# Two semaphore signals of TensorE in each attention step, scores ahead of the next keys, and ten buffers for 0/1 matrices

## The reference

```
q_i = (x @ idx_wq).reshape(B_, L_, N_IDX_HEAD, D_HEAD)
k_i = x @ idx_wk
s_i = jax.nn.relu(jnp.einsum('bthd,bsd->bths', q_i, k_i))
I = jnp.einsum('bths,h->bts', s_i, idx_w)
...
_, idx = jax.lax.top_k(I, kk)
...
key_c = (c_kv @ W_uk)[bi, idx].reshape(B_, L_, kk, N_HEAD, D_HEAD)
value = (c_kv @ W_uv)[bi, idx].reshape(B_, L_, kk, N_HEAD, D_HEAD)
...
scores = (jnp.einsum('bhld,bhlkd->bhlk', q_c, k_c) + jnp.einsum('bhld,blkd->bhlk', q_r, key_r)) * scale
attn = jax.nn.softmax(scores.astype(jnp.float32), axis=-1).astype(v.dtype)
out = jnp.einsum('bhlk,bhlkd->bhld', attn, v)
...
return out @ W_out
```

## Time and profile before

| | |
|---|---|
| time, 3 runs | 932.55 us median (932.08 to 933.81) |
| the profiled execution | 933.06 us, span 931.2 us in the trace |
| busy share of the span | PE 90%, DVE 73%, ACT 55%, POOL 53% |
| costliest group of POOL | L621, the gathers into the ring, 284.6 us in 284 instructions |
| the chain that ended last | PE 51%, POOL 17%, DVE 12%, issue 10%, ACT 6%, DMA 2% |
| mean granted clock of TensorE | 0.91 of full speed |

### The profile page before, as it was taken

How to read it: one execution, slowest core, us unless ns; L and a number is a source line. 1 busy time by engine, 2 the same in 40 slices (tenths; PEclk the granted TensorE clock), 3 DMA queues, 4 the chain that set the end, 5 groups by cost and what they waited for, 6 DMA issues and landing times.

```text
span 931.2 us, 17728 instructions
## 1 busy us (share of the span) xinstructions
PE 837.1 (90%) x5742; PEld 489.5 (53%) x5742; DVE 679.2 (73%) x1979; ACT 508.3 (55%) x1463; POOL 492.2 (53%) x738
## 2 busy tenths in 40 slices
PE   6867999999999999999999998778989987889786
PEld 3334556565556565656565654445549532535353
DVE  1879899788698998999899986413222279686864
ACT  5455756654567788877877854434432244243231
POOL 4620038877757777777777777777410425202120
PEclk9768999999999999999999986857597999899898
DMA  7310122222101111111111111191025200000000
GB/s 246 73 23 1 30 49 57 46 54 48 36 20 28 29 24 31 26 24 30 27 26 26 29 24 29 23 256 24 21 75 162 54 18 0 1 0 12 11 1 23
DMA packets 59642, 39.98 MB, mean 43 GB/s; under 512 B 27072, under 2 KB 51360, under 8 KB 59424
## 3 DMA queue, kind: packets, MB, share of 16 engines
q1 hardware_dynamic: 44064, 23.40, 10.0%
q0 software_dynamic: 12800, 14.15, 7.6%
q10 hardware_dynamic: 2688, 1.31, 0.5%
HBM read 33.31 MB, written 5.55 MB: 42 GB/s over the span
## 4 chain that ended last, share of the span: by engine, by line
PE 51%; POOL 17%; DVE 12%; issue 10%; ACT 6%; DMA 2%; SPq 0%; POOLq 0%; DVEq 0%; ACTq 0%
POOL G L621 11%; PE psK L745 6%; PE psI L655 6%; PE psS L1753 3%; PE psK L641 3%; PE psP L807 3%; ACT R L903 2%; PE psP L814 2%; PE psS L781 2%; PE psP L796 2%; POOL spacer L620 2%; PE psS L784 2%; POOL w_first L621 2%; DVE G L1971 2%; PE psM L718 1%
## 5 line engine op out<-in xcount | busy, mean ns | idle before, releaser
L621 POOL DMA_INDIRECT G<-key_rows,idx x284 | 284.6, 1002 | 180.0 <-DVEq L1142 82.6
L655 PE MATMUL psI<-kiT,qiT 64*128 64x512 f32 (+5 forms) x320 | 91.7, 595 | 16.1 <-ACT R L903 15.8
L641 PE MATMUL psK<-cst 128*128 128x512 bf16 x315 | 93.7, 408 | 4.9 <-ACT KT L1007 4.9
L1031 ACT ACTIVATE PT<-psP 128x256 f32<-128x256 f32 x128 | 48.4, 378 | 88.5 <-PE psP L814 86.4
L999 ACT ACTIVATE PR<-PR,rinv 128x208 f32<-128x208 f32 x128 | 58.7, 459 | 69.6 <-DVE rinv L1319 69.3
L1115 DVE SCALAR_TENSOR_TENSOR SC<-R,w_i,SC 128x512 f32<-128x512 f32 (+5 forms) x120 | 78.4, 654 | 5.5 <-ACT R L903 2.6
L1145 DVE MAX8 top<-SC 128x8 f32<-128x128 f32 (+15 forms) x64 | 78.5, 1226 | 2.3
L903 ACT ACTIVATE R<-psI 128x512 f32<-128x512 f32 (+5 forms) x160 | 73.3, 510 | 11.5 <-PE psI L655 10.0
L1147 DVE FIND_INDEX8 idxf<-top,SC 128x8 uint32<-128x128 f32 (+15 forms) x64 | 78.3, 1223 | 0.0
L1259 DVE TENSOR_TENSOR G<-G,rank_tab 128x256 f32<-128x256 f32 x75 | 31.1, 415 | 55.2 <-DMA G<-key_rows,idx 55.1
L1548 POOL TENSOR_SCALAR rstd<-mv 128x4 f32<-128x4 f32 x12 | 3.1, 256 | 128.8 <-DVE mv L1944 128.8
(11 more groups left out here) (348 smaller groups left out, 1887.6 us busy)
## 6 DMA issues: line engine op xcount, KB each, us to landing
G<-key_rows,idx POOLq DMA_INDIRECT x284, 2.5
rtmp<-idx_rows SPq DMA_DIRECT2D x32, 128.0 KB
xslots<-zrow SPq DMA_DIRECT2D x4, 320.0 KB, 9.2
SC<-xslots SPq DMA_DIRECT2D x8, 160.0 KB
yslots<-SC ACTq DMA_DIRECT2D x8, 160.0 KB, 2.6
V<-val_rows SPq DMA_DIRECT2D x15, 80.0 KB
xr<-in_x SPq DMA_DIRECT2D x1, 1024.0 KB, 9.4
qiT<-in_w_gate SPq DMA_DIRECT2D x4, 256.0 KB, 4.5
```

The lines of the kernel that those rows point to most:

```text
L621: pool.indirect_dma_start(ring[o % RING][:, g % GPB, DR:], None, key_rows, bass.IndirectOffsetOnAxis(ap=idx[:, t, g:g + 1], axis=0),).then ...
L641: pe.matmul(ps[:, :].rearrange("p (a n) -> p a n", a=2), warm_w, warm_x, start=True, stop=True, skip_group_check=True)
L655: pe.matmul(psI[i][:, 0:w], lhs, kiT[64 * i:64 * i + 64, CH * c:CH * c + w], start=True, stop=True).then_inc(s["i_mm"], 1)
```

## The change

TensorE now signals twice in a step. `pe_a` rises once behind `p_transpose` and `weighted` (and what stood at the end of the step before, now called `tail(n-1)`), and `pe_b` once behind scores and keys. The thirteen semaphores of the kinds of work are gone (`i_mm` stays for the first tiles), and every reader waits for the `pe_a` or `pe_b` of the step in which its input is made. The order of the two parts behind `weighted` is exchanged: the scores of block n-1 come first, then the keys of block n. y of tile t moves from the middle of step 8(t+2) to the end of step 8(t+2)-1, ahead of `pe_b`, with waits for `s_min` and `vs_cp` in place of the wait for `y_mm` (only y of tile 15 stays). `NOH` goes from 6 to 10: four more buffers for 0/1 matrices lie in `ot_region`; and `key_match` no longer waits for the single 0/1 matrix that lay in its buffer, but for `pe_b` of the block before.

```
-NVS, NOH = 7, 6
+NVS, NOH = 7, 10
...
-                   for i in range(NOH)]
+                   for i in range(6)]
+        one_hot += [ot_region[:, NH * P + CH // 2 * i:NH * P + CH // 2 * (i + 1)].bitcast(BF16) for i in range(NOH - 6)]
...
+        LAST_Y = NB * (NT + 1) - 1
+        Y_AT = {NB * (t + 2) - 1: t for t in range(NT - 1)}
...
+        a_steps = [n for n in range(N0, N1 + 1) if tail_of(n - 1) or LAG_T <= n < NT * NB + LAG_W]
+
+        def first_half(n):
+
+            return sum(1 for m in a_steps if m <= n)
+
+        def second_half(n):
+
+            return min(max(n + 1, 0), NT * NB + LAG_S)
```

TensorE (in `scores`, then the loop):

```
-                    if b == NB - 1 and t >= 1:
-                        out_project(t - 1)
-                        pe.wait_ge(s["y_mm"], t)
...
-                for n in range(N0, N1):
-                    st, b = divmod(n, NB)
-                    keep_warm(psK, WARM_TAIL.get(n - NT * NB, 0))
+                for n in range(N0, N1 + 1):
+                    mm = tail(n - 1)
+                    if n < N1:
+                        keep_warm(psK, WARM_TAIL.get(n - NT * NB, 0))
                     if 0 <= n - LAG_T < NT * NB:
-                        p_transpose(n - LAG_T)
+                        mm = p_transpose(n - LAG_T)
                     if 0 <= n - LAG_W < NT * NB:
-                        weighted(n - LAG_W)
+                        mm = weighted(n - LAG_W)
+                    if n in a_steps:
+                        mm.then_inc(s["pe_a"], 1)
                     if n == 1:
                         rank_transpose()
+                    mm = None
+                    if 0 <= n - LAG_S < NT * NB:
+                        mm = scores(n - LAG_S)
                     if 0 <= n < NT * NB:
-                        front(n)
-                    if 0 <= n - LAG_S < NT * NB:
-                        scores(n - LAG_S)
+                        mm = front(n)
+                    if n in Y_AT:
+                        pe.wait_ge(s["s_min"], n - 1)
+                        if (n - 4) // NB in ONE_HOT:
+                            pe.wait_ge(s["vs_cp"], hot_order(n - 4) + 1)
+                        mm = out_project(Y_AT[n])
+                    if mm is not None:
+                        mm.then_inc(s["pe_b"], 1)
```

The readers that the prediction speaks of:

```
 def relu_pair
+                    if n is None:
+                        act.wait_ge(s["i_mm"], m + 1)
+                    else:
+                        act.wait_ge(s["pe_a"], first_half(n + 1))
...
-                        act.wait_ge(s["i_mm"], 2 * m + i + 1)
...
 def k_copy
-                    act.wait_ge(s["k_t"], ring_order(n) + 1)
-                    if n >= 2:
-                        act.wait_ge(s["s_mm"], n - 1)
+                    act.wait_ge(s["pe_b"], second_half(n))
...
 def key_match
+                    if m >= 2:
+                        dve.wait_ge(s["pe_b"], second_half(hot_block[m - 2]))
...
-                        if o >= NOH:
-                            dve.wait_ge(s["oh_mm"], o - NOH + 1)
...
 def key_rank
-                    dve.wait_ge(s["oh_mm"], hot_tiles(n + 1))
+                    dve.wait_ge(s["pe_b"], second_half(n))
...
 def s_minimum
-                    dve.wait_ge(s["s_mm"], n + 1)
+                    dve.wait_ge(s["pe_b"], second_half(n + LAG_S))
```

More of the change, by code:

```diff
@@ L408, in program @@
             w_mm w_cp kproj kproj_cp rope_p lat_row key_l mu lrot kr_out val_out g_rot lT lT_cp rope rope_a
[L409 to L412, removed]
+            i_mm i_relu i_first comb im topk idx_ready q_e q_chain qf_a q_cp
+            pe_a pe_b k_ev s_min p_exp p_cp orec p_nrm o_cp v_ld
+            bn ln_a x1_n x1d x1_cp lg_e rt_a rt lg_cp rte plc slots_ready ld_l1
+            kb oh vs_cp ix_w""".split()
         s = {n: sem("s_" + n) for n in names}
@@ L707, in q_project @@
                         pe.wait_ge(s["q_cp"], 2 * t)
-                    pe.matmul(psM[:, :], cqT[:, P * t:P * (t + 1)], w_q[:, :], start=True,
-                              stop=True).then_inc(s["q_mm"], 1)
+                    return pe.matmul(psM[:, :], cqT[:, P * t:P * (t + 1)], w_q[:, :], start=True, stop=True)
                 def q_transpose(t, j):
@@ L843, in cumulate @@
                               skip_group_check=True)
-                    pe.matmul(PX[:, E0:2 * E0], ones, ohsum[:, :], start=False, stop=True,
-                              skip_group_check=True).then_inc(s["cum_mm"], 1)
-                for n in range(N0, N1):
-                    st, b = divmod(n, NB)
-                    keep_warm(psK, WARM_TAIL.get(n - NT * NB, 0))
+                    return pe.matmul(PX[:, E0:2 * E0], ones, ohsum[:, :], start=False, stop=True,
+                                     skip_group_check=True)
@@ new lines, in tail @@
+                def tail(n):
+                    mm = None
+                    for t, u in index_pairs.get(n, ()):
+                        mm = index_pair(t, u)
+                    if n in QT_AT:
+                        mm = q_transpose(*QT_AT[n])
+                    if n in Q_AT:
+                        mm = q_project(Q_AT[n])
+                    if n == LAST_Y:
+                        mm = out_project(NT - 1)
+                    if n in TILE_AT["x1_t"]:
+                        mm = x1_transpose(TILE_AT["x1_t"][n])
+                    if n in TILE_AT["router"]:
+                        mm = router(TILE_AT["router"][n])
+                    if n in TILE_AT["cumulate"]:
+                        mm = cumulate(TILE_AT["cumulate"][n])
+                    return mm
@@ L980, in q_evac @@
                 def q_evac(t, j):
-                    act.wait_ge(s["q_t"], 2 * t + j + 1)
+                    act.wait_ge(s["pe_a"], first_half(q_transpose_step(t, j) + 1))
                     if t >= 2 and j == 0:
-                        act.wait_ge(s["s_mm"], NB * (t - 1))
+                        act.wait_ge(s["pe_b"], second_half(NB * (t - 1) - 1 + LAG_S))
                     act.activation(Q[:, t % 2, :, 4 * j:4 * j + 4].rearrange("p q h -> p h q"),
@@ L1321, in add_inputs @@
                 def add_inputs(t):
-                    dve.wait_ge(s["y_mm"], t + 1)
+                    if t < NT - 1:
+                        dve.wait_ge(s["pe_b"], second_half(NB * (t + 2) - 1))
+                    else:
+                        dve.wait_ge(s["pe_a"], first_half(LAST_Y + 1))
                     dve.tensor_tensor(xa[:, :], PY, xr[:, t, :], ALU.add).then_inc(s["bn"], 1)
```

109 lines of the change are left out of this document (48 added, 61 removed).

## The result

The changed kernel takes 955.62 us (median of 4 runs, 953.08 to 958.28) against 933.18: ratio 1.0241, 95% interval 1.0209 to 1.0272. It is slower, as forecast, but by 22.4 us where the sum said 6.65.

A forecast was written before the change was run, and what follows sets the result against it. GpSimd's gathers bound the kernel from tile 8 on, with TensorE, then VectorE setting their start. Terms of 7.85 less 1.2 gave +6.65 on 933.06, so 939.7, or 939.2 as median; range 936 to 942.

The forecast's parts named there:

- the sum: Whole kernel: 7.85 us later to the indices of tile 8, less 1.2 at the end, gives +6.65.
- The bound: GpSimd's gathers from tile 8 on, 5.98 us per block; delays before 275.93 move everything behind one for one.
- the rival of 925: Stretch 200 to 250: VectorE's pace rules, so 6.4 us of buffer waits and 1.2 come back; 925.4, chance 0.13.
- The step that failed: Steps where TensorE paces: exchanging scores and keys costs nothing; 1.08 us only when the pace passes from VectorE to TensorE.
- Slower still: Rival: TensorE runs slower behind new stops, 8.4 us at most, 2.8 counted, giving 942.0; chance 0.10.
- three stops: TensorE stops at the start of steps 13, 21 and 27, where it was without a stop.
- Its 14%: Slowdown assumed behind each TensorE stop, from the scores part taking 1.23 us for 1.08 at the attention's end.
- The 20 us behind each stop: Length of slower TensorE running assumed behind each of three stops: 3 x 20 x 0.14 = 8.4 us at most.
- S or y ahead of `key_rank` at a hand-over: Before tile 8's indices: `key_rank` also waits for the scores part (1.08 us) or y (1.2 in step 39).
- the terms from step 15 on: Steps 15 to 17 cost +1.9 us, steps 21 to 39 +3.35, lost overlap of matmuls +0.5.
- The start: First `relu_pair` now also waits for the query transposes, so the head sum comes +1.0 us later.
- The tail: Behind the last gathered rows: scores of block 126 now done while TensorE waits for the rows, -1.2 us.

The follow-up runs named there:

- order alone: Kernel before with only scores and keys exchanged, signals apart, six buffers: 963.93 us for 933.24, ratio 1.0339.
- keys first: Changed kernel with keys of block n ahead of scores of block n-1 again: 943.86 us for 934.32, ratio 1.0095; at 1180, ratio 0.9996.
- copy earlier: Changed kernel with ScalarE's copy of the values moved ahead of p_norm and exps: 955.82 us for 932.76, ratio 1.0271.
- order and buffers: Kernel before with scores ahead of keys and ten 0/1-matrix buffers, all signals apart: 952.96 us for 933.48, ratio 1.0225.
- run 24: Not a run label: the text reads "In this run 24% of the chain", a percentage, said of the second run of keys first.

## Why the prediction was wrong

**The bound** was read rightly: everything up to the indices of tile 8 moved the end one for one, the stretch of 64 gathered blocks hid the rest at 5.99 us each, GpSimd waited no more than 0.3 us at a time for the ring in it and not for indices, and VectorE's leg behind block 39 kept its 20.5 us. The waits at `key_match` went into those at `key_rank`, also as said, so the rival of 925 is out. (In the changed code `key_match` waits for `pe_b` of the block two before, `hot_block[m - 2]`, not of the block before.)

**The step that failed** is "Where TensorE paces step after step, the exchange of scores and keys costs nothing, since the same sum passes between two `key_rank`s". It put the exchange at nothing there, looked only at the work of TensorE, and at one of the scores' waits, that for `key_rank`. In the view of the changed kernel no stop of TensorE waits for `key_rank`; 13.8 us wait for the copy. The scores have others, above all the one for `values_copy`, which stands in ScalarE's order behind p_norm, exps and, in some steps, work that waits for VectorE. Before, the keys (1.4 to 3.4 us in this stretch) ran between the weighted sums and the scores and covered it; now the keys themselves stand behind the stop. I costed covers for what was moved off the path, and not for the waits of the part that moved forward. The order alone is 1.034, and with scores first TensorE stands 16.8 to 18.8 us behind 125, where it had stood 0.3; of that, moving the copy took away 6.5 us, and 6.0 of the delay. That the order is the cause is shown; that the rest of these stops has the same reason is read from the waits, and no run takes them away one by one.

**The rival that came true was undersized.** "Slower still" put the clock at 2.8 us, 8.4 at most, with three stops. There were more stops, and the granted clock took 20 us more up to tile 8 than before, over half of it behind 125 (0.94 for 1.00). Its 14% compared unlike parts: the 1.08 of the earlier trace rows holds `values_transpose`, and the part that the tail has too starts at 202.53, so 203.26 - 202.53 = 0.73 stands against 1.23, which is 68% more. Behind the stop shown above the matmuls took twice as long. The 20 us behind each stop came from no row. Nor is there one price for each stop: with keys first, 6.7 us idle behind 125 left the clock at 1.00.

**The terms of the sum** mostly belong to another part than I gave them to. S or y ahead of `key_rank` at a hand-over is a cost of the joint signal in either order. With keys first the way from the indices of tile 5 to those of tile 8 was 11.0 - 5.4 = 5.6 us longer, where the terms from step 15 on sum to 5.75 (1.9 + 3.35 + 0.5), and 21 waits at `key_rank` end with the scores or y; in the changed kernel 4 waits, 9.0 us, end with y. The sizes agree, but no run at 933 takes the joint signal away, so this part is argued and not shown. The start, +1.0 for relu, was 1.5 (L1148 at 68.24 for 66.74), but the indices of tile 5 came 5.4 us late with keys first and 7.8 in the changed kernel, where I had 2.1, with a clock of 0.75 to 0.76 for 0.89 from 60 to 125. Why the clock is lower there, with less standing still and with keys first too, is not settled.

**The tail**, -1.2 for S of 126: the order is as said, but the 11 us that came back are mostly the clock. From the last gather to the last weighted sum the traces have 25.2 (before), 24.4 (keys first), 25.0 (copy earlier), 20.3 (order alone), 18.8 (order and buffers) and 18.4 us (changed), at clocks of 0.61, 0.61, 0.64, 0.92, 0.95 and 0.97. Before:

```profile
658.40:683.60 25.20, 24.49 (x155) 14.95 (x153) 5.33 (x36) 11.27 (x44) 6.12 (x6) 0.61 0.06 16
```

6.8 of the 11 us are in this stretch. Long ones occur in either order, so it is not the order by itself; what decides it stays open. So some 7 us of the measured time are luck of the tail: with the clock of before there, the change would have cost nearer 29 than 22 us (an estimate: 22.4 + 6.8).

**Signals.** The kernel with this order and ten buffers takes 952.96 us with all signals apart and 955.62 with joint ones and y moved. About 200 signals fewer did not make it faster. The Trainium skill, "TensorE: Matmul & The Clock Gate", section "The cost: per-tile semaphore tail", would give an estimated 5.3 us for them; its figure is for small matmuls packed side by side in the array. Neither this pair nor the distances of the earlier trace rows show it.

## What to carry to other kernels

When a part of an in-order engine's work is moved forward, list every wait of that part, not only those of the part that it passes, and ask what ran ahead of it while they were met. A joint signal makes the first reader wait for the last work under it (here 24.6 and 8.3 us of `key_rank`'s waits with keys first): keep a signal of its own for the reader on the path, and join only those that have time. Read an experiment at the place where the cost arises (here the gathers of tile 8) as well as in its time, since a later stretch can give it back or take it for another reason.

## What was not expected of the hardware

**A stop can cost twice.** Behind a stop of 2.72 us the same matmuls follow at 0.43 for 0.215 us. The mean clock of the whole span, 0.91 before and 0.90 after, hides it.

**The same tail in 18.4 or 25.0 us**, at clocks of 0.97 and 0.64, with the same work and 1.4 and 0.8 us of idle time of TensorE.

**Late instructions of TensorE.** Where the kernel before took 1136 to 1184 us, TensorE's rows look like this (keys first, second run):

```profile
163.48 0.21 PE L836 MATMUL psP<-PT,xT 128*32 128x32 f32 x1 [0.52 <-issue]
164.89 0.21 PE L836 MATMUL psP<-PT,xT 128*32 128x32 f32 x1 [1.19 <-issue]
166.31 0.21 PE L836 MATMUL psP<-PT,xT 128*32 128x32 f32 x1 [1.21 <-issue]
167.74 0.21 PE L836 MATMUL psP<-PT,xT 128*32 128x32 f32 x1 [1.22 <-issue]
```

Matmuls that otherwise stand 8 in 0.42 us come 1.4 us apart, and the view names no signal that they wait for. In this run 24% of the chain that ended last is put down to "another core or an unknown queue", and in the kernel before at 933 nothing. One and the same chip was in this condition in some sets and not in others, so it is no property of a chip; its cause was not found.
